# Attention of a macaron block on one core: spectra with tokens on the partitions, the running sum made by TensorE, and three chunks in flight instead of two

## What is computed

```python
def _L0_attn_ref(x, Wq, Wk, Wv):
    q = jnp.einsum('bsd,ed->bse', x, Wq)
    k = jnp.einsum('bsd,ed->bse', x, Wk)
    v = jnp.einsum('bsd,ed->bse', x, Wv)
    fk = jnp.fft.rfft(k, axis=-1)
    fk = fk / (jnp.abs(fk) + EPS)
    fq = jnp.fft.rfft(q, axis=-1)
    fq = fq / (jnp.abs(fq) + EPS)
    fv = jnp.fft.rfft(v, axis=-1)
    fkv = jnp.cumsum(fk * fv, axis=-2)
    values_hat = jnp.fft.irfft(fkv * jnp.conj(fq), n=D, axis=-1)
    return x + values_hat
...
x = x + 0.5 * _L0_ffn_ref(_layernorm(x), ...)
x = x + _L0_attn_ref(_layernorm(x), L0_attn_Wq, L0_attn_Wk, L0_attn_Wv)
x = x + 0.5 * _L0_ffn_ref(_layernorm(x), ...)
```

## Time and profile before

| | us |
|---|---|
| median of 3 runs (2047.5 to 2054.9) | 2049.3 |
| the profiled execution | 2060.44 |
| its span | 2058.6 |
| last weight subtraction to the last X addition of the attention | 706.54 to 1301.30 |
| TensorE, VectorE, ScalarE, GpSimd busy, share of the span | 78%, 69%, 33%, 37% |

### The profile page before, as it was taken

One profiled execution on the slowest core, in us unless ns is written; L12 is line 12 of the kernel. 1 busy time (PEld: TensorE's weight loads), 2 busy tenths in 40 slices (PEclk: granted clock), 3 DMA queues, 4 the chain that ended last, 5 costly groups with the idle time before them and its releaser, 6 DMA issues.

```text
span 2058.6 us, 35171 instructions
## 1 busy us (share of the span) xinstructions
PE 1597.5 (78%) x9854; PEld 1381.3 (67%) x9855; DVE 1419.2 (69%) x3362; ACT 672.2 (33%) x1126; POOL 766.7 (37%) x868
## 2 busy tenths in 40 slices
PE   2899999589999466767767674489999976999940
PEld 1777777489999355555555563377777766999940
DVE  4788888545555368888898888377788763555557
ACT  3334343134444133232323131233433412444410
POOL 0444444225454223333333232044444432555420
PEclk9999999889999767776777676599999987999975
DMA  8211111144444301010101000011111114444459
GB/s 276 82 53 42 55 50 47 53 120 143 140 142 135 96 22 41 21 41 20 41 20 41 20 20 0 31 54 51 45 50 55 42 44 114 140 138 143 136 194 349
DMA packets 123782, 170.36 MB, mean 83 GB/s; under 512 B 14881, under 2 KB 105394, under 8 KB 123442
## 3 DMA queue, kind: packets, MB, share of 16 engines
q1 hardware_dynamic: 89938, 91.05, 15.5%
q0 software_dynamic: 25344, 70.29, 9.3%
q10 hardware_dynamic: 8448, 8.39, 1.2%
HBM read 91.03 MB, written 81.89 MB: 84 GB/s over the span
## 4 chain that ended last, share of the span: by engine, by line
PE 47%; DVE 18%; issue 12%; DMA 10%; POOL 7%; ACT 3%; SPq 2%; POOLq 0%; DVEq 0%; ACTq 0%
PE bank L613 14%; PE bank L614 12%; PE bank L615 12%; POOL lists L407 6%; DMA lists<-a_rows,a_slots 5%; PE bank L739 3%; PE bank L749 3%; DVE t_rn L1149 2%; DMA f_yf<-results 2%; DVE t_cum L1167 2%; ACT a_rows L503 2%; DVE a_gate_u L987 1%; PE bank L843 1%; DVE X L1230 1%; DVE t_pr L1165 1%
## 5 line engine op out<-in xcount | busy, mean ns | idle before, releaser
L418 POOL DMA_INDIRECT results<-b_yb,b_goal x272 | 261.6, 962 | 343.6 <-DVE b_yb L1090 298.4
L407 POOL DMA_INDIRECT lists<-a_rows,a_slots x256 | 259.8, 1015 | 117.5 <-issue 64.5
L613 PE MATMUL bank<-t_xah,t_wfh 128*128 128x512 f32 x192 | 115.0, 599 | 113.6 <-DVE t_xal L864 64.1
L1090 DVE COPY b_yb<-bank 128x512 f32<-128x512 f32 x136 | 94.0, 691 | 147.9 <-PE bank L615 147.9
L613 PE MATMUL bank<-a_sw2h,a_uh 128*128 128x256 f32 x512 | 155.4, 304 | 42.7 <-DVE a_xtl L864 35.7
L613 PE MATMUL bank<-ew_h,b_xbth 128*128 x544 | 166.7, 306 | 1.1 <-DVE b_xbtl L864 1.0
L613 PE MATMUL bank<-ew_h,b_hth 128*128 x544 | 155.9, 287 | 7.5 <-DVE b_htl L864 3.0
L457 ACT ACTIVATE a_uh<-a_gate_u 128x512 fp32r<-128x512 f32 x128 | 77.1, 624 | 245.9 <-PE bank L615 193.0
L614 PE MATMUL bank<-ew_l,b_xbth 128*128 x544 | 154.1, 283 | 0.0
L615 PE MATMUL bank<-ew_h,b_xbtl 128*128 x544 | 153.8, 283 | 0.0
L615 PE MATMUL bank<-ew_h,b_htl 128*128 x544 | 152.4, 280 | 0.0
(11 more groups left out here) (212 smaller groups left out, 4882.2 us busy)
## 6 DMA issues: line engine op xcount, KB each, us to landing
b_xb<-lists SPq DMA_DIRECT2D x272, 132.0 KB
t_yg<-results SPq DMA_DIRECT2D x32, 512.0 KB, 4.6
f_yf<-results SPq DMA_DIRECT2D x32, 512.0 KB, 10.9
X<-in_L_attn_x SPq DMA_DIRECT2D x16, 512.0 KB, 4.1
out<-X ACTq DMA_DIRECT2D x16, 512.0 KB, 7.1
results<-b_yb,b_goal POOLq DMA_INDIRECT x272
w_raw_ew<-in_L_ffn_ew SPq DMA_DIRECT2D x2, 2048.0 KB, 13.8
lists<-a_rows,a_slots POOLq DMA_INDIRECT x256, 2.4
```

The lines of the kernel that those rows point to most:

```text
L407: pool.indirect_dma_start(out=lists, out_offset=bass.IndirectOffsetOnAxis(ap=slots[:, q, k, j:j + 1], axis=0), in_=rows[:, q, j, :], in_of ...
L418: pool.indirect_dma_start(out=results, out_offset=bass.IndirectOffsetOnAxis(ap=goal[:, slot, blk:blk + 1], axis=0), in_=YB[:, slot, blk, : ...
L613: pe.matmul(o, a("h"), b("h"), start=first, stop=False)
L1090: dve.tensor_copy(YB[:, slot].rearrange("p b d -> p (b d)"), bank[:, 7 - par, :]).then_inc(s_yok, 1)
```

## The change

The attention is written anew with the tokens on the partitions.

- A spectrum is 4 tiles of 256 columns: 129 cosine columns, then 127 sine columns, the Nyquist frequency in the place of the first sine. The input is now the stationary operand and the weights move (24 products of 256 columns for 12 of 512). The whole separate path of the 129th frequency is gone. The powers and the reciprocals are 4 x 129 columns; products of complex parts use the 127 columns that have both.
- K times V has no scan. GpSimd makes three running sums over tiles (PX), and TensorE makes the sum along tokens: per tile a product of the triangle with KV and one of the ones matrix with the sum of the earlier tiles, both plain f32, 256 columns, into banks 6 and 7.
- VectorE multiplies that sum, read from PSUM, by Q (PP, TA, TB), TensorE transposes the product (8 transposes), ScalarE and VectorE make the halves from PSUM, and TensorE makes the inverse transform into banks 6 and 7 as well.
- The steps run over more chunks: results are combined for chunk s+2, spectra made for s, product and running sum for s-1, inverse for s-2, addition to X for s-3.
- The raw weights lie in another place than YG, and SyncE's wait before the first load of results is gone, with the load of the sign row.

Cut to its core, with the leading blanks of the functions left out; where a removed line is not shown, it stands in the function above. The parts are, in this order, the constants, SyncE, GpSimd, ScalarE, TensorE and VectorE.

```diff
-    fwd = np.zeros((D, NW), np.float32)
+    fwd = np.zeros((D, D), np.float32)
     fwd[:, :NF] = np.cos(ang)
-    fwd[:, NF:D] = -np.sin(ang)
-    fwd[:, D] = 1.0 - 2.0 * (np.arange(D) % 2)
+    fwd[:, NF:] = -np.sin(ang)
+    fwd[:, NF] = 1.0 - 2.0 * (np.arange(D) % 2)
...
+    inv[NF] = (1.0 - 2.0 * (np.arange(D) % 2)) / D
...
-sp.dma_start(raw_sign[:], c_sign).then_inc(s_mat, 16)
-sp.wait_ge(s_mlo, 3)
...
 def attention(s, par, half):
-    now, nxt = inside(s, CH), inside(s + 1, CH)
+    prev, now, nxt, far = inside(s - 1, CH), inside(s, CH), inside(s + 1, CH), inside(s + 2, CH)
+    def power_sum():
+        return pool.tensor_tensor(SQ[:, :, 1:NF], SQ[:, :, 1:NF], SQ[:, :, NF + 1:], ALU.add)
+    if prev:
+        pool.wait_ge(s_qev, s)
+        power_sum().then_inc(s_qsum, 1)
+        pool.wait_ge(s_kvd, s)
+        atleast(pool, s_cps, s - 1)
...
+            ch.link(pool.tensor_tensor(PX[:, 1, :], KV[:, 0, :], KV[:, 1, :], ALU.add))
+            ch.settle()
+            ch.link(pool.tensor_tensor(PX[:, 2, :], PX[:, 1, :], KV[:, 2, :], ALU.add))
+            ch.settle()
+            pool.tensor_tensor(PX[:, 3, :], PX[:, 2, :], KV[:, 3, :], ALU.add).then_inc(s_px, 1)
...
+        pool.wait_ge(s_qinv, s)
+        ch.link(pool.tensor_tensor(FQ[:, :, 0:NF + 1], FQ[:, :, 0:NF + 1], RQ[:], ALU.mult))
+        pool.tensor_tensor(FQ[:, :, NF + 1:], FQ[:, :, NF + 1:], RQ[:, :, 1:NF], ALU.mult).then_inc(s_qn, 1)
     if now:
...
+        pool.wait_ge(s_kev, s + 1)
+        power_sum().then_inc(s_ksum, 1)
+    if far:
+        rstd_of(par, s + (CH + 3))
     if nxt:
-        rstd_of(1 - par, s + (CH + 2))
         pool.wait_ge(s_txn, s + 2)
         xc = X[:, bass.ds((s + 1) * J, J), :]
         pool.tensor_tensor(xc, xc, XN[:], ALU.add).then_inc(s_add, 1)
...
 def attention(s, par, half):
-    now, nxt = inside(s, CH), inside(s + 1, CH)
+    prev, now, nxt = inside(s - 1, CH), inside(s, CH), inside(s + 1, CH)
+    def magnitude(to):
+        return act.activation(to, SQ[:, :, 0:NF + 1], ACT.Sqrt)
+    if inside(s - 2, CH):
+        act.wait_ge(s_ptp, s - 1)
+        atleast(act, s_aps, s * 2 - 4)
+        copy(VH["h"][:], bank[:, 0:2, :]).then_inc(s_ph, 1)
+    if prev:
+        act.wait_ge(s_qsum, s)
+        atleast(act, s_qn, s - 1)
+        magnitude(RQ[:]).then_inc(s_qroot, 1)
     if now:
...
+        act.wait_ge(s_kps, s + 1)
+        atleast(act, s_vused, s)
+        atleast(act, s_qroot, s)
+        k_ps = bank[:, 2:4, :].rearrange("p b (j d) -> p (b j) d", j=2)
+        ca.link(copy(FK[:], k_ps))
+        act.activation(SQ[:], k_ps, ACT.Square).then_inc(s_kev, 1)
     if nxt:
         act.wait_ge(s_rstd, s + (CH + 2))
         atleast(act, s_add, s + 1)
                                  scale=rstd[:, 1 - par, j:j + 1])
         ins.then_inc(s_txn, 1)
     if now:
...
+        act.wait_ge(s_ksum, s + 1)
+        magnitude(SQ[:, :, 0:NF + 1]).then_inc(s_kroot, 1)
+        act.wait_ge(s_qps, s + 1)
+        atleast(act, s_cused, s)
+        q_ps = bank[:, 2:4, :].rearrange("p b (j d) -> p (b j) d", j=2)
+        ca.link(copy(FQ[:], q_ps))
     if nxt:
         act.wait_ge(s_atp, s + 2)
         atleast(act, s_qps, s + 1)
         copy(XA["h"][:], bank[:, 0:2, :]).then_inc(s_ah, 1)
...
     if now:
...
+        act.wait_ge(s_kn, s + 1)
+        act.activation(SQ[:], q_ps, ACT.Square).then_inc(s_qev, 1)
...
 def attention(s, par, half):
...
+    prev, now, nxt, old = inside(s - 1, CH), inside(s, CH), inside(s + 1, CH), inside(s - 2, CH)
+    def spectrum(i, to):
+        for j in range(J):
             for k in range(KD):
...
+                ins = three(bank[:, to + j // 2, (j % 2) * D:(j % 2 + 1) * D],
+                            lambda h: XA[h][:, k, j * P:(j + 1) * P], lambda h: WF[h][:, k, i, :],
+                            k == 0, k == KD - 1)
+        return ins
     if now:
...
+        if isinstance(s, int) and s == 0:
+            pe.wait_ge(s_mlo, 3)
+        pe.wait_ge(s_al, s + 1)
+        atleast(pe, s_qev, s)
+        spectrum(0, 2).then_inc(s_kps, 1)
+    if prev:
+        pe.wait_ge(s_kvd, s)
+        pe.wait_ge(s_px, s)
+        atleast(pe, s_aout, s * 2 - 4)
+        before = [None, KV[:, 0, :], PX[:, 1, :], PX[:, 2, :]] if par == 1 else [PX[:, (j + 3) % 4, :]
+                                                                                for j in range(J)]
+        for j in range(J):
+            o = bank[:, 6 + j // 2, (j % 2) * D:(j % 2 + 1) * D]
+            ins = pe.matmul(o, tri_f, KV[:, j, :], start=True, stop=before[j] is None)
+            if before[j] is not None:
+                ins = pe.matmul(o, ones_f, before[j], start=False, stop=True)
+        ins.then_inc(s_cps, 1)
+    if now:
+        atleast(pe, s_vused, s)
+        spectrum(1, 4).then_inc(s_vps, 1)
+        pe.wait_ge(s_kev, s + 1)
+        spectrum(2, 2).then_inc(s_qps, 1)
     if nxt:
         pe.wait_ge(s_txn, s + 2)
...
-        atleast(pe, s_aout, s * 2)
+        atleast(pe, s_pl, s - 1)
         for k in range(KD):
             for j in range(J):
                 ins = pe.transpose(bank[:, k, j * P:(j + 1) * P], XN[:, j, k * P:(k + 1) * P], ident)
         ins.then_inc(s_atp, 1)
...
+    if old:
+        pe.wait_ge(s_pl, s - 1)
+        if prev:
+            pe.wait_ge(s_cused, s)
+        else:
+            pe.wait_ge(s_aout, s * 2 - 4)
         for half_ in range(2):
             for i in range(2):
                 j = 2 * half_ + i
...
                 for r in range(2):
...
+                    ins = three(bank[:, 6 + half_, i * D:(i + 1) * D],
+                                lambda h: VH[h][:, r, j * P:(j + 1) * P], lambda h: WI[h][:, r, :],
+                                r == 0, r == 1)
             ins.then_inc(s_aps, 1)
+    if prev:
+        pe.wait_ge(s_p, s)
+        if nxt:
+            pe.wait_ge(s_al, s + 2)
+        else:
+            atleast(pe, s_pl, s - 1)
+        for r in range(2):
+            for j in range(J):
+                ins = pe.transpose(bank[:, r, j * P:(j + 1) * P], PP[:, j, r * NF:(r + 1) * NF], ident)
+        ins.then_inc(s_ptp, 1)
...
 def attention(s, par, half):
...
+    prev, now, nxt, far = inside(s - 1, CH), inside(s, CH), inside(s + 1, CH), inside(s + 2, CH)
+    lo, hi = slice(1, NF), slice(NF + 1, D)
+    if prev:
+        dve.wait_ge(s_qroot, s)
+        ch.link(dve.tensor_scalar(RQ[:], RQ[:], FFT_EPS, None, ALU.add))
+        ch.settle()
+        dve.reciprocal(RQ[:], RQ[:]).then_inc(s_qinv, 1)
+    if inside(s - 2, CH):
+        dve.wait_ge(s_ph, s - 1)
+        low(VH["l"][:], bank[:, 0:2, :], VH["h"][:]).then_inc(s_pl, 1)
+    if inside(s - 3, CH):
+        dve.wait_ge(s_add, s - 2)
+        for h in range(2):
+            dve.wait_ge(s_aps, s * 2 + (h - 5))
+            xc = X[:, bass.ds(s * J + (2 * h - 3 * J), 2), :]
+            dve.tensor_tensor(xc, xc, bank[:, 6 + h, :].rearrange("p (j d) -> p j d", j=2),
+                              ALU.add).then_inc(s_aout, 1)
+    if far:
+        c = s + 2
         dve.wait_ge(s_yg, c * 32 + 32)
         for k in range(TOPK):
             for j in range(J):
...
                 ch.settle()
         dve.wait_ge(s_comb, c + 1)
         apart(dve)
...
+        stats(c, par)
+    if prev:
+        c_ps = bank[:, 6:8, :].rearrange("p b (j d) -> p (b j) d", j=2)
+        dve.wait_ge(s_cps, s)
+        dve.wait_ge(s_qn, s)
+        ch.link(dve.tensor_tensor(PP[:], c_ps, FQ[:], ALU.mult))
+        ch.link(dve.tensor_tensor(TA[:], c_ps[:, :, lo], FQ[:, :, hi], ALU.mult))
+        dve.tensor_tensor(TB[:], c_ps[:, :, hi], FQ[:, :, lo], ALU.mult).then_inc(s_cused, 1)
+        ch.settle()
+        ch.link(dve.tensor_tensor(PP[:, :, lo], PP[:, :, lo], PP[:, :, hi], ALU.add))
+        ch.settle()
+        dve.wait_ge(s_cused, s)
+        dve.tensor_tensor(PP[:, :, hi], TB[:], TA[:], ALU.subtract).then_inc(s_p, 1)
     if now:
...
         dve.wait_ge(s_kroot, s + 1)
...
+        mag = SQ[:, :, 0:NF + 1]
+        ch.link(dve.tensor_scalar(mag, mag, FFT_EPS, None, ALU.add))
+        ch.settle()
+        ch.link(dve.reciprocal(mag, mag))
+        ch.settle()
+        ch.link(dve.tensor_tensor(FK[:, :, 0:NF + 1], FK[:, :, 0:NF + 1], SQ[:, :, 0:NF + 1], ALU.mult))
+        dve.tensor_tensor(FK[:, :, hi], FK[:, :, hi], SQ[:, :, lo], ALU.mult).then_inc(s_kn, 1)
+        ch.settle()
+        dve.wait_ge(s_kn, s + 1)
+        v_ps = bank[:, 4:6, :].rearrange("p b (j d) -> p (b j) d", j=2)
+        dve.wait_ge(s_vps, s + 1)
+        if prev:
+            dve.wait_ge(s_p, s)
+        ch.link(dve.tensor_tensor(KV[:], FK[:], v_ps, ALU.mult))
+        ch.link(dve.tensor_tensor(TA[:], FK[:, :, lo], v_ps[:, :, hi], ALU.mult))
+        dve.tensor_tensor(TB[:], FK[:, :, hi], v_ps[:, :, lo], ALU.mult).then_inc(s_vused, 1)
     if nxt:
         dve.wait_ge(s_ah, s + 2)
         low(XA["l"][:], bank[:, 0:2, :], XA["h"][:]).then_inc(s_al, 1)
     if now:
...
+        ch.settle()
         dve.wait_ge(s_vused, s + 1)
...
```

(26 more changed lines are left out.)

200 lines of the change are left out of this document (43 added, 157 removed).

## The result

| | before | after |
|---|---|---|
| median of 4 runs each, us | 2049.6 (2047.5 to 2054.9) | 1975.5 (1974.0 to 1976.6) |
| ratio after / before | | 0.963, 95% interval 0.9615 to 0.9654 |
| profiled execution (its span), us | 2060.44 (2058.6) | 1975.29 (1973.5) |
| last weight subtraction to last X addition, us | 706.54 to 1301.30, 594.8 | 706.40 to 1223.96, 517.6 |

The forecast was 1971 us with a range of 1945 to 2015. The gain lies where it was looked for: the stretch is 77.2 us shorter, and the medians differ by 74.1.

What follows compares the result with a forecast made beforehand. VectorE was taken as nearest its limit: a turn of 25.2 work + 2.3 + 2.9 + 0.2 waits + 0.2 handoffs = 30.8 us. The stretch, 28 + 113.1 + 338.8 + 36 = 516 against 594.8, gave 1971 us, range 1945 to 2015.

Steps and rivals of the forecast that it cites:

- The stretch: From the last weight subtraction to the last X addition, between the two expert stages: 516 us forecast against 594.8 before.
- Its start: From the last weight subtraction to the first K reciprocal: 28 us forecast, 11 sooner than the 39.2 of before.
- The wait for the root: VectorE idle 2.3 us a turn for ScalarE's Q magnitude, behind the input subtraction, eight transposes and ScalarE's copy.
- The collision at the SBUF-only addition: VectorE's addition of the Q product runs one behind the other with GpSimd's addition to X: cost 1.9 us a turn.
- The one at the combination: GpSimd's K power sum falls on VectorE's combination of the next chunk: cost 1.0 us a turn.
- The running sum: TensorE's 7 or 8 plain f32 products take 6.4 or 3.3 us; VectorE's wait costs 0 to 0.9, taken as 0.2.
- the first of the two scans: VectorE's running-sum scan in the old turn, counted as 2.41 us that goes, and half of that for the other.
- TensorE: Array work taking 22 to 24 of a 30.8 us turn at a clock of 0.71, hidden behind VectorE.
- (a): Rival, fewer stalls: collisions miss and the array is warm, turn 28.5 us, 1936 to 1946, up to 1954; chance 0.15.
- (b): Rival: GpSimd pays for rows cut to 127 of 256 columns, 1 to 2 us a turn, 1986 to 2001; chance 0.13.
- (c): Rival: TensorE's array stays at the low clock through the whole stretch, turn 34.8 us, 2043 us; chance 0.07.
- (d): Rival: TensorE's running sum is the bound at two times L787's pace, turn 41 us, 2136 us; chance 0.05.

## Why the forecast held, point by point

**The stretch** was put at 516 us and is 517.6. Its start: 28 forecast, 28.8 measured (706.40 to 735.2). The turns: 113.1 + 338.8 = 451.9 forecast, 454.0 measured. The end: 36 forecast, 34.8 measured. The first turn took 27.56 us (27.5 in the prediction), a middle one 30.85 (30.8).

That the start came out is partly luck. The terms written down for it add up to 26.5 us with the epsilon addition, so 1.5 of the 28 have no source. The trace has as much in a collision that the prediction did not count, since it looked for collisions only at instructions with two sources:

```profile
732.51 2.37 POOL L460 TENSOR_TENSOR X<-X,t_xn 128x1024 f32<-128x1024 f32 x1
733.21 1.96 DVE L1177 TENSOR_SCALAR t_sq<-t_sq 128x516 f32<-128x516 f32 x1 [2.83 <-ACT t_sq L565]
```

The first epsilon addition for K takes 1.96 us instead of 0.42.

**The terms of the turn.** The wait for the root: 2.3 forecast, 2.47 measured, by the chain that the order had shown, and worth 2.7 when taken away. The collision at the SBUF-only addition: 1.9 forecast, 2.1 measured. The one at the combination: 1.0 and 1.0. The running sum: 0.2 forecast, 0 in a full turn; it took 5.4 us there (904.40 to 909.79), within the 3.3 to 6.4. VectorE waited for it only at the end (17.9 us in four waits up to the last turn), where leaving half of it out gave 2.2 us net. VectorE's own work: 30.85 - 2.47 - 3.1 = 25.3, against 25.2 and 0.2 of handoffs.

**A term whose size was right for the wrong reason** was the first of the two scans. They did go with 2.41 and 1.2 us, but half of the first was a collision with GpSimd. The sum was not hurt, because the new turn was counted from its own instructions and not as the old one less what went. A reckoning by difference would have had to know it.

**TensorE** was overestimated. 22 to 24 us of busy time a turn stood in the prediction; the three windows above give 96.75 of 150 us, 19.9 of a turn of 30.85. The sum had taken a granted clock of 0.71, and it is 0.83, 0.86 and 0.76. Its running sum and the spectra around it, in windows of 2 us:

```profile
905.00:907.00 2.00, 2.00 (x6) 1.64 (x5) 1.95 (x3) 0.64 (x1) 0.87 (x1) 0.50 0.00 0
909.00:911.00 2.00, 2.00 (x16) 1.92 (x15) 1.85 (x9) 0.00 (x0) 0.00 (x0) 1.00 0.30 60
923.00:925.00 2.00, 0.00 (x0) 0.00 (x0) 2.00 (x3) 0.00 (x0) 1.06 (x1) 0.50 0.00 0
```

The running sum begins at the low level (0.50 is 1.2 GHz), behind 4.5 us in which TensorE waited for the X additions; by the V spectrum the clock is at its full level, and stays there over the next transposes (915.37, eight in 1.03 us) and the inverse; after the idle time behind them it is down again. The first products of the sum are 0.86 us apart and the last 0.43, as the rows of the weight products had given. The error had no effect on the time, since TensorE is hidden either way.

**From the profile to the median** is where most of the 4.5 us of error lies. I took the 11.1 us by which the profiled execution of before lay above its median as lying wholly outside the stretch, so that all 79 us counted. The stretches differ by 77.2, which is 1.8 of the error, and the medians by 74.1, which is 3.1 more; 2049.3 - 79 is 1970.3 besides, and I wrote 1971. From the last X addition to the span's end the execution of before took 757.3 us (2058.6 - 1301.30), the changed kernel 749.5 and the seven others 746.7 to 753.3, with the same code there. Some 4 to 11 of the 11.1 us were there, then; that the rest was in the stretch fits, and is not shown.

**The rivals.** (a), fewer stalls, did not happen by itself, but its direction was right: the stalls could be had, as three of the kernels show. (b), strided rows dear on GpSimd: the multiplications and sums of 508 or 516 columns take 1.17 to 1.26 us alone, less than the contiguous 1.28 of the earlier trace rows. (c), the low clock throughout, is out by the windows. The Trainium skill, page "TensorE: Matmul & The Clock Gate", section "Part 4: PE-mode transpose", had spoken for it; here 16 transposes a turn stand beside a clock of 0.76 to 0.86. Only eight of the 16 stand behind idle time, as the prediction had all of them: these begin at the low level (925.44, 1.94 us), while the eight between products run at the full one. Whether transposes alone would raise the clock, no run here shows. (d), the running sum as the bound, is out by its pace and by the kernel without its second product.

## What to carry to other kernels

Count the new turn from its own instructions, each from a row of the same shape, and only then add what it waits for; the old turn's durations may hold collisions. Before moving an instruction of GpSimd, ask what VectorE runs at the new place: in these runs it cost nothing beside a reciprocal or an operation that reads PSUM, while beside one with both sources in SBUF, or the addition of a constant, the pair ran one behind the other. When a change is in, look at every short instruction that stands behind a long wait in one engine's order: here one swap on ScalarE and one wait on GpSimd brought 68 us more, nearly as much as the change itself.
